# A two-layer graph-attention kernel: GpSimd's additions moved around a layer norm, and the second turn written out in an order of its own

## The reference

```python
# layer 0: pre-norm transformer block, 8 heads of 32, MLP of 1024
nx = _ln(x, ln1_g, ln1_b)
q, k, v = (nx @ wq + bq), (nx @ wk + bk), (nx @ wv + bv)       # as 8 heads
bias = where(adj > 0, 0.1 * adj * adj, -inf)
attn = softmax(einsum('bhqd,bhkd->bhqk', q, k) / sqrt(32) + bias)
x1 = x + (einsum('bhqk,bhkd->bhqd', attn, v) @ wo + bo)
x2 = x1 + gelu(_ln(x1, ln2_g, ln2_b) @ w1 + b1) @ w2 + b2
# layer 1: one head of 256, no MLP, norm at the end
w = softmax(where(adj == 0, -inf, (x2 @ Wq) @ (x2 @ Wk).T / sqrt(256)))
out = layer_norm(x2 + (w @ (x2 @ Wv)) @ Wo + bo, gamma, beta)
```

## Time and profile before

| what | us |
|---|---|
| median of 3 runs | 931.99 |
| lowest, highest | 927.68, 933.8 |
| the profiled execution's own time | 936.33 |
| its span, first to last instruction | 934.5 |
| PE busy | 872.8 (93% of the span) |
| VectorE, ScalarE, GpSimd busy | 697.4, 605.6, 503.8 |

### The profile page before, as it was taken

The page is one execution under the profiler, slowest core; times in us unless marked ns, Lnnn a source line. Parts: engine busy times, 40 slices in busy tenths (PEclk is TensorE's granted clock), DMA queues, the critical chain, the costliest instruction groups (busy, mean ns, idle before and its releaser), DMA issues.

```text
span 934.5 us, 22040 instructions
## 1 busy us (share of the span) xinstructions
PE 872.8 (93%) x7159; PEld 778.7 (83%) x7159; DVE 697.4 (75%) x2522; ACT 605.6 (65%) x1830; POOL 503.8 (54%) x374
## 2 busy tenths in 40 slices
PE   8998669999999999999999999999999999999896
PEld 8786459798888979888897988889798888989796
DVE  6686557878787877777787777778778787876646
ACT  5684746666767676676767667576766767584642
POOL 3532543746756464666646466664646656463512
PEclk9899779999999999999999999999999999999999
DMA  8100251523233252414324241432524143243001
GB/s 260 35 2 13 68 158 47 159 77 110 85 99 127 57 164 70 157 34 112 111 62 159 72 154 37 111 109 62 158 75 149 41 109 121 56 136 114 1 24 34
DMA packets 106304, 87.11 MB, mean 93 GB/s; under 512 B 3462, under 2 KB 91164, under 8 KB 106268
## 3 DMA queue, kind: packets, MB, share of 16 engines
q1 hardware_dynamic: 106252, 86.66, 30.8%
q10 hardware_dynamic: 16, 0.00, 0.0%
HBM read 47.85 MB, written 38.80 MB: 93 GB/s over the span
## 4 chain that ended last, share of the span: by engine, by line
PE 70%; DVE 7%; issue 5%; ACT 3%; DMA 1%; POOL 1%; DVEq 0%; SPq 0%; POOLq 0%
PE bank L401 20%; PE bank L403 19%; PE bank L402 19%; PE bank L562 3%; PE bank L718 3%; PE bank L586 3%; ACT p L1025 2%; DVE pT L1326 2%; DVE nx L1271 2%; PE bank L668 1%; DVE p L1398 1%; PE bank L497 1%; DMA p_s<-parked 1%; PE bank L711 1%; DVE mv L1261 1%
## 5 line engine op out<-in xcount | busy, mean ns | idle before, releaser
L961 ACT ACTIVATE p_s<-bank,neg_max 128x128 f32<-128x128 f32 x464 | 162.5, 389 | 90.8 <-DVE neg_max L1303 86.6
L1801 POOL TENSOR_TENSOR p_s<-p_s,rsum 128x512 f32<-128x512 f32 x116 | 118.1, 1041 | 189.6 <-DVE rsum L1310 189.6
L401 PE MATMUL bank<-w_hi,hT_hi 128*128 128x256 f32 x512 | 147.9, 289 | 1.3 <-DVE hT_lo L1195 1.3
L403 PE MATMUL bank<-w_hi,hT_lo 128*128 128x256 f32 x512 | 144.2, 282 | 0.0
L402 PE MATMUL bank<-w_lo,hT_hi 128*128 128x256 f32 x512 | 144.1, 282 | 0.0
L1303 DVE CUSTOM_DVE_ANT_0 bank<-bank,bias 128x128 f32<-128x128 f32 x464 | 117.5, 329 | 4.0 <-PE bank L562 3.8
L401 PE MATMUL bank<-n2T_hi,w_hi 128*128 128x512 f32 (+1 forms) x272 | 109.5, 403 | 7.6 <-DVE hT_lo L1195 7.6
L992 ACT ACTIVATE bank<-bank,vec_cols 128x512 f32<-128x512 f32 (+1 forms) x136 | 86.6, 637 | 34.0 <-PE bank L403 28.2
L961 ACT ACTIVATION_READ_ACCUMULATOR p_s<-bank,neg_max 128x1 f32 x464 | 106.4, 229 | 0.0
L402 PE MATMUL bank<-n2T_lo,w_hi 128*128 128x512 f32 (+1 forms) x272 | 104.6, 385 | 0.0
L403 PE MATMUL bank<-n2T_hi,w_lo 128*128 128x512 f32 (+1 forms) x272 | 104.6, 385 | 0.0
(11 more groups left out here) (233 smaller groups left out, 2494.8 us busy)
## 6 DMA issues: line engine op xcount, KB each, us to landing
parked<-pT SPq DMA_DIRECT2D x116, 256.0 KB, 4.0
pT<-parked SPq DMA_DIRECT2D x15, 1024.0 KB, 5.4
p_s<-parked SPq DMA_DIRECT2D x14, 1024.0 KB, 7.6
xs<-in_x SPq DMA_DIRECT2D x15, 512.0 KB, 3.8
out<-y SPq DMA_DIRECT2D x14, 512.0 KB, 2.9
adj_i<-in_adj SPq DMA_DIRECT2D x15, 256.0 KB, 2.7
out<-y SPq DMA_DIRECT2D x3, 256.0 KB, 2.2
x2T_f<-in_L_gnn_w SPq DMA_DIRECT2D x1, 512.0 KB, 6.8
```

The source lines that it names most:

```text
L401: mm(out, a_hi, b_hi, start=first, stop=False)
L403: return mm(out, a_lo, b_hi, start=False, stop=last)
L961: last = run(to, of, ACT.Exp, scale=-1.0, bias=neg_max[:, r, place:place + 1], accum_out=psum[:, r, place:place + 1])
L1801: P.tensor_tensor(p_s[:, r, :, :], p_s[:, r, :, :], rsum[:, r, :, None].to_broadcast([128, 4, NODES]), ALU.mult).then_inc(pool_p, 1)
```

## The change

GpSimd's program of `turn` and VectorE's are reordered around norm 2, and the second turn becomes a function of its own on PE, ScalarE, VectorE and GpSimd. SyncE's program stays as it is, and no instruction's size changes: the same work is done in another order.

```diff
--- before.py
+++ after.py
...
     n2_transpose(1, True)
     p1_transpose(0)
-    scores(2, 1)
     project_v(2, 1)
     attend1_pairs(0)
+
+def second_turn():
+    for j in range(HT):
+        mlp_up(1, j, True)
+    scores(2, 1)
+    mlp_down(1, 0)
+    mlp_down(1, 1)
+    norm_transpose(3)
+    project_k(3, 0)
+    project_k(3, 1)
+    x2_transpose(1)
+    project_q(3, 0)
+    project_q(3, 1)
+    t_project(1)
+    attend(2, 0)
+    attend(2, 1)
+    scores(3, 0)
+    out_project(2, 0)
+    out_project(2, 1)
+    project_v(3, 0)
+    scores1(1)
+    vo_project(1, 0, True)
+    vo_project(1, 1, True)
+    scores(3, 1)
+    n2_transpose(2, True)
+    p1_transpose(1)
+    project_v(3, 1)
+    pe.wait_ge(act_vo, 2)
+    attend1(1, 0)
+    pe.wait_ge(dve_vo, 1)
+    pe.wait_ge(act_v, pair0(3) + 2)
+    attend1(1, 1)
...
     q_copy(2, 0)
     q_copy(2, 1)
     t_copy(0)
+    exps1(0)
+    vo_copy(0)
     exps(2, 0, 0)
-    exps(2, 0, 1)
-    exps1(0)
-    exps(2, 0, 2)
-    exps(2, 0, 3)
-    vo_copy(0)
     n2T_copy(1)
     p1T_copy(0)
-    exps(2, 1, 0)
-    exps(2, 1, 1)
+    exps(2, 0, 1)
+    exps(2, 0, 2)
     v_copy(2, 1)
-    exps(2, 1, 2)
...
+def second_turn():
+    run(probe[:, :], minus_half[:, 0:1], ACT.Gelu)
+    for j in range(HT):
+        gelu(1, j)
+    run(probe[:, :], minus_half[:, 0:1], ACT.Exp)
+    for r in range(HPT):
+        exps(2, 1, r)
+    nxT_copy(3)
+    k_copy(3, 0)
+    k_copy(3, 1)
+    for t in range(KT):
+        x2T_copy(1, (t,))
+        x2T_high(1, (t,))
+    q_copy(3, 0)
+    q_copy(3, 1)
+    t_copy(1)
+    attn_high(2, 0)
+    attn_high(2, 1)
+    exps(3, 0, 0)
+    exps(3, 0, 1)
+    exps(3, 0, 2)
+    v_copy(3, 0)
+    exps(3, 0, 3)
+    vo_copy(1)
+    exps1(1)
+    exps(3, 1, 0)
+    n2T_copy(2)
+    p1T_copy(1)
+    exps(3, 1, 1)
+    v_copy(3, 1)
+    exps(3, 1, 2)
+    exps(3, 1, 3)
...
-    if isinstance(ga, int) and ga == 2:
-        for r in range(HPT):
-            blocks(ga, 1, r)
...
     residual1(ga, 0, True)
     x2T_low(gb)
     residual1(ga, 1, True)
-    if whole:
-        inverse(gp, 1, 2)
     sums2(ga, 0)
     sums2(ga, 1)
     if whole:
-        inverse(gp, 1, 3)
+        inverse(gp, 1, 2)
+    moments(2, ga)
+    if whole:
         blocks(gp, 1, 0)
     t_copy(gb)
-    moments(2, ga)
+    if whole:
+        inverse(gp, 1, 3)
+    norm2(ga)
     if whole:
         blocks(gp, 1, 1)
-        blocks(gp, 1, 2)
-    norm2(ga)
     biased1(gb)
     if whole:
+        blocks(gp, 1, 2)
+    vo_copy(gb)
+    if whole:
         blocks(gp, 1, 3)
-    vo_copy(gb)
     n2T_low(ga)
...
     biased(2, 0, 0)
+    biased1(0)
     norm2(1)
-    biased1(0)
-    biased(2, 0, 1)
-    biased(2, 0, 2)
-    biased(2, 0, 3)
     inverse_sums1(0)
+    for r in range(1, HPT):
+        biased(2, 0, r)
     n2T_low(1)
+    residual3(0, 0)
     for r in range(HPT):
         inverse(2, 0, r)
-    biased(2, 1, 0)
-    biased(2, 1, 1)
+
...
+def second_turn():
+    sums1(3)
+    moments(1, 3)
     blocks(2, 0, 0)
     blocks(2, 0, 1)
-    biased(2, 1, 2)
-    biased(2, 1, 3)
-    residual3(0, 0)
+    h_low(1, 0)
+    norm1(3)
+    h_low(1, 1)
     blocks(2, 0, 2)
     blocks(2, 0, 3)
+    h_low(1, 2)
+    sums3(0)
+    h_low(1, 3)
+    moments(3, 0)
+    h_low(1, 4)
+    h_low(1, 5)
+    norm3(0)
+    h_low(1, 6)
+    h_low(1, 7)
+    for r in range(HPT):
+        biased(2, 1, r)
+    residual2(1, 0)
     for r in range(HPT):
         inverse(2, 1, r)
+        if r:
+            blocks(2, 1, r - 1)
+    blocks(2, 1, 3)
+    residual2(1, 1)
+    nxT_low(3)
+    x2T_low(1)
+    t_copy(1)
+    attn_low(2, 0)
+    attn_low(2, 1)
+    for r in range(HPT):
+        biased(3, 0, r)
+    inverse(3, 0, 0)
+    residual1(2, 0, True)
+    inverse(3, 0, 1)
+    blocks(3, 0, 0)
+    residual1(2, 1, True)
+    sums2(2, 0)
+    sums2(2, 1)
+    inverse(3, 0, 2)
+    moments(2, 2)
+    inverse(3, 0, 3)
+    blocks(3, 0, 1)
+    norm2(2)
+    biased1(1)
+    vo_copy(1)
+    blocks(3, 0, 2)
+    blocks(3, 0, 3)
+    for r in range(HPT):
+        biased(3, 1, r)
+    n2T_low(2)
+    inverse_sums1(1)
+    for r in range(HPT):
+        inverse(3, 1, r)
+    residual3(1, 0)
+    residual3(1, 1)
+    for r in range(HPT):
+        blocks(3, 1, r)
...
     x_plus_bo(2)
-    for r in range(HPT):
-        normal(2, 0, r)
-    for r in range(HPT):
-        normal(2, 1, r)
     x1_plus_b2(1)
     mask1(1)
     move_up(2)
+    for r in range(HPT):
+        normal(2, 0, r)
+
+def second_turn():
+    rstd(1, 3)
+    pool.wait_ge(ln_dve[1], ln_end(3))
+    adjacency(3)
+    edges(3)
+    rstd(3, 0)
+    gain(0, 2)
+    offset(0, 2)
+    bias(3)
+    for r in range(HPT):
+        normal(2, 1, r)
+    x2_plus_bo(1)
+    for r in range(HPT):
+        normal(3, 0, r)
+    rstd(2, 2)
+    pool.wait_ge(ln_dve[2], ln_end(2))
+    x_plus_bo(3)
+    x1_plus_b2(2)
+    mask1(2)
+    move_up(3)
+    for r in range(HPT):
+        normal(3, 1, r)
 
 def turn(gp, ga, gb, gc):
     rstd(1, gp)
@@ -1828,13 +1959,17 @@
     rstd(3, gc)
     gain(gc, size(gc))
     offset(gc, size(gc))
-    for q in pairs(gp):
-        for r in range(HPT):
-            normal(gp, q, r)
-    x_plus_bo(gp)
+    for r in range(HPT):
+        normal(gp, 0, r)
+    x2_plus_bo(gb)
+    if size(gp) > 2:
+        for r in range(3):
+            normal(gp, 1, r)
     rstd(2, ga)
     pool.wait_ge(ln_dve[2], ln_end(ga))
-    x2_plus_bo(gb)
+    if size(gp) > 2:
+        normal(gp, 1, 3)
+    x_plus_bo(gp)
     x1_plus_b2(ga)
     mask1(ga)
     move_up(gp)
```

More of the change, by code:

```diff
@@ L882, in _ @@
             first_turn()
-            turn(3, 2, 1)
+            second_turn()
             with pe.Fori(3, GROUPS - 2) as g:
@@ L1099, in first_turn @@
                 t_copy(0)
+                exps1(0)
+                vo_copy(0)
                 exps(2, 0, 0)
-                exps(2, 0, 1)
-                exps1(0)
-                exps(2, 0, 2)
-                exps(2, 0, 3)
-                vo_copy(0)
                 n2T_copy(1)
                 p1T_copy(0)
-                exps(2, 1, 0)
-                exps(2, 1, 1)
+                exps(2, 0, 1)
+                exps(2, 0, 2)
                 v_copy(2, 1)
-                exps(2, 1, 2)
-                exps(2, 1, 3)
+                exps(2, 0, 3)
+            def second_turn():
[30 more added lines that the diff above has]
+                exps(3, 1, 3)
             def last_turn(ga, gb):
@@ L1689, in _ @@
             first_turn()
-            turn(3, 2, 1, 0)
+            second_turn()
             with dve.Fori(3, GROUPS - 2) as g:
```

## The result

The changed kernel takes 895.66 us (median of four runs, 894.95 to 897.54), the kernel before 930.66 us (four runs, 927.68 to 933.8): a ratio of 0.9627, 95% interval 0.9589 to 0.9664, faster by 35 us. The forecast was 901 us, its range 888 to 917.

What follows compares the result with a forecast made beforehand. PE bounds the loop, with one wait before `n2_transpose`. From 936.33 us, 28.3 for the loop (12 x 1.37 + 8 x 1.48) and 5.5 for the second turn come off, then half of 4.3: 901 us, range 888 to 917.

Steps and rivals of the forecast that it cites:

- The loop's mechanism: Loop turn: with `rstd` ahead of `x_plus_bo`, PE's 1.77 us wait before `n2_transpose` shrinks to 0.4, 1.37 us gained per turn.
- twice over: Norm 2 in the loop: a GpSimd addition both holds back VectorE's `ve` and stands ahead of `rstd` in the queue.
- The half clock: Loop: PE's clock stays whole without the long wait, another 1.48 us in each of eight slow turns.
- The half of the 4.3 us: Whole kernel: taken off because the profiled execution lay 4.3 us above the median and other runs may have fewer slow turns.
- The second turn: Second turn with the end of the first: 17.2 us of waits removed, 11.6 put in, 5.5 us gained (0 to 11).
- The waits that are put in: Second turn: new PE waits at up products 1.8, `project_k` 2.1, `project_v` 2.4, `attend1` 2.6, next head 2.7; 11.6 us.
- those that I had as gone: Second turn and first turn's end: up products' 7.6 us, two waits for `parked` 5.4, and 4.2; 17.2 us removed.
- the 4.2 us: End of the first turn: PE's two longest waits there, to be relieved by `exps1` earlier and `scores(2, 1)` later.
- The load of x: Loop: x, issued later, lands in 3.8 us, ahead of the stores, leaving 0.4 us of cover before `sums1`, 7 before.
- The second turn giving nothing: Rival: the loop's 28.3 us alone, 908 us, or 907 with the median's share; chance 14 in 100.
- the wait only moving: Rival: in the loop `scores1` slips by 1.8 us instead of 0.4, so about 929 us; chance 7 in 100.
- x late, somewhat or behind the stores: Two rivals, loop: x 1.5 us late, 914 us, 11 in 100; x behind the stores, 944 us (slower), 6 in 100.

Runs made afterwards that it cites:

- e5: Changed kernel with GpSimd's `x_plus_bo` put back ahead of the `rstd` of norm 2, the rest of the new order kept: 917.78 us.
- e12: Kernel before with two steps of GpSimd's turn exchanged, `rstd` of norm 2 and its wait ahead of `x_plus_bo`, nothing else: 907.06 us.
- e4: Kernel before with only the loop's turns in the new order on GpSimd and VectorE, first and second turn old: 904.76 us.
- e3: Changed kernel with the loop's turns in the old order on GpSimd and VectorE, new second turn and first turn's tail kept: 920.39 us.
- e6: Changed kernel with GpSimd's `x_plus_bo` one place further back, behind `x1_plus_b2`, so the next x loads later: 918.81 us.
- e1: Changed kernel with GpSimd's loop turn in the old order, VectorE's left in the new one: 973.59 us.
- e11: Changed kernel with VectorE's loop turn in the old order and GpSimd's `x_plus_bo` directly behind `rstd` of norm 2: 935.23 us.

## Why the prediction was right

**The loop's mechanism: right.** e5 and e12 show it from both sides: the 2.37 us of `x_plus_bo` ahead of `rstd` are PE's wait. That the addition also holds `ve` is so in the kernel before, but it does not cost "twice over" as the prediction has it: `rstd` stands behind the addition in any case, and in e5 PE waits 1.73 us with a `ve` that is not held by it. The turn was forecast at 51.73 us and takes 51.49. The gain per turn is 1.61 us, not 1.37: `scores1` slips by 0.1 us instead of 0.4, since the sums come 0.3 us earlier (I had 0.16) and `t_copy` ends 0.5 later (I had 0.86). 12 x 0.24 = 2.9 us more.

**The half clock: right in kind, too large in size.** 8 x 1.48 = 11.8 us was counted from one execution, which had eight slow turns. By e4 the loop gains 24.3 us on the average run, of which 12 x 1.61 = 19.3 are the wait; 5 us are left for the clock (0.7 to 9.3 by e4's interval), three or four turns in twelve. e12 gives some more: 22.2 us less 12 x 1.20 for its wait leaves 7.8. The half of the 4.3 us that I took off for this was too little. (902.5 less that half is 900.4; the forecast's 901 is rounded up.)

**The second turn: near in size, made up otherwise.** 5.5 us were forecast (0 to 11). e3 measures 8.7 (5.8 to 11.7), but not all of that need be the second turn's. At the attend of group 3 the eight profiles with the new second turn stand at 184.9 us on average and the three with the old one (before, e4, e12) at 191.2, so 6.2 us apart; and e3's profile has no slow loop turn where that of before has eight. What is left of the 8.7 can be loop turns that kept their clock; the runs without a profile do not tell. The waits that are put in came as counted: 11.6 us forecast; measured 2.1 at the up products (0.57 and 1.57), 1.6 at `project_k`, 2.0 at `project_v`, 2.5 at `attend1` and 3.0 at the next head (2.11 and 0.93), 11.2 in all. Of those that I had as gone, one for `parked` is still there with 2.0 us, and at 84 to 100 us two new ones of 1.4 and 1.2 us stand where the 4.2 us were. So the waits gave less than I counted, and the clock gave the rest. From 84 us to the attend of group 3, before and after:

```profile
84.00:192.07 108.07, 87.55 (x633) 74.39 (x632) 74.91 (x285) 67.44 (x211) 56.11 (x44) 0.89 0.32 96
84.00:184.68 100.68, 84.43 (x634) 70.69 (x632) 71.08 (x285) 67.11 (x211) 56.22 (x44) 0.97 0.35 103
```

PE is idle for 20.5 us before and for 16.3 after, and busy for 87.6 and 84.4 us with the same work: of the 7.4 us between these two profiles 4.3 are waits and 3.1 busy time, at a clock of 0.97 instead of 0.89. Busy times of the kernel before:

```profile
88.00:102.00 14.00, 8.26 (x66) 7.10 (x65) 9.76 (x60) 8.49 (x41) 5.84 (x6) 0.76 0.12 40
102.00:125.00 23.00, 15.41 (x57) 11.47 (x56) 17.35 (x54) 16.07 (x50) 16.95 (x14) 0.78 0.22 57
125.00:142.00 17.00, 11.63 (x125) 9.14 (x124) 4.52 (x9) 7.23 (x12) 3.68 (x4) 0.81 0.66 202
```

and of the changed one:

```profile
88.00:102.00 14.00, 10.89 (x61) 8.91 (x60) 11.12 (x57) 13.12 (x49) 12.01 (x10) 1.00 0.14 40
102.00:125.00 23.00, 19.71 (x161) 17.37 (x160) 17.98 (x64) 14.84 (x47) 14.44 (x13) 1.00 0.22 57
125.00:142.00 17.00, 14.85 (x158) 11.97 (x158) 5.30 (x20) 7.40 (x16) 2.40 (x1) 1.00 0.64 202
142.00:164.00 22.00, 17.33 (x127) 15.17 (x127) 16.96 (x88) 15.20 (x75) 15.27 (x12) 0.84 0.27 73
```

The clock (the number behind GpSimd's) was 0.76 to 0.81 up to 142 us and is 1.00 there now; from 142 to 164 us, among the new waits, it is 0.84 where it was 0.99. I had named the clock only as a way to lose. That it gave the 3.1 us is the reading of these stretches; no run changed the clock alone.

**The load of x: right, by luck of 0.3 us.** Forecast cover 0.4 us, measured 0.1. x took 4.1 us with the stores right behind it, not 3.8, but its issue came 0.3 us earlier than forecast, so it landed 34.6 us after the turn's attend as forecast. The cover shrank because `sums1` comes 0.2 us earlier, with the shorter turn. Neither shift was foreseen, nor the 0.3 us that x takes longer beside the stores, where the prediction let a load issued first keep its 3.8. e6 shows that the place decides as feared: 2.2 us late cost 23 us in all.

**The rivals.** The second turn giving nothing falls by e3 and by the attends; the wait only moving falls by the loop, in which PE has no wait left; x late, somewhat or behind the stores, did not happen (`sums1` has no idle time before it), and e6 is what it would have looked like.

## What to carry to other kernels

Ask of each long instruction on a helper engine what short one stands behind it in the queue, and who waits for that one: here two steps exchanged brought 22 of 35 us. An order on one engine is only as good as the order on the engine that it talks to: with the second turn the same, one of the loop's two halves alone loses 53 us against the old order (e1 and e3), and the other alone gains half of what both do per turn. And price an instruction's place from both sides: what it holds when it is early, and what (a load, a buffer) it holds back when it is late.

## What was not expected of the hardware

- A `tensor_scalar` of 128x4 on VectorE, 0.17 us with GpSimd idle (e12), took 1.64 us beside a GpSimd addition and 0.66 beside a multiplication: it ends when that instruction ends. The Trainium skill (SBUF — State Buffer, section "Who interferes with whom") states that VectorE in some modes and GpSimd share a port pair that the first holds for its whole instruction; these durations agree with it.
- The length of a short wait alone does not tell whether the clock falls: behind 1.7 to 1.8 us of idle time PE lost it in eight turns of twelve in one profile, in none of e3's and in one of eleven in e5's, and behind 1.9 us in six of eleven in e11's. Behind 4.2 us (e1) it ran at half each time. What decides it was not found. The profiled execution of before thus holds 11.8 us of lost clock, where e4 and e12 leave some 5 to 8 for the average run.
